# First cross-attention of a two-layer block: queries repeated on four 32-row bands, softmax sums from ACT's accumulator

## What is computed

```python
Ql = (Q @ Wq.T + bq).reshape(b, tq, H, HD).transpose(0, 2, 1, 3)
Kl = (K @ Wk.T + bk).reshape(b, tk, H, HD).transpose(0, 2, 1, 3)
scores = jnp.einsum('bhqd,bhkd->bhqk', Ql, Kl) / scale
scores = jnp.where(key_padding_mask[:, None, None, :], neg_inf, scores)
attn = jax.nn.softmax(scores, axis=-1)
out = jnp.einsum('bhqk,bkd->bqhd', attn, V).reshape(b, tq, H * dv)
return out @ Wo.T + bo
...
x = x + _L0_xattn_ref(_layernorm(x, axis=-1), ctx_1024, ctx_1024, ...)
x = x + _L0_ffn_ref(_layernorm(x, axis=-1), ...)
x = x + _L1_xattn_ref(_layernorm(x, axis=-1), ctx_1024, mask_BxS_ik0, ...)
x = x + _L1_ffn_ref(_layernorm(x, axis=-1), ...)
```

## Time and profile before

| | us |
|---|---|
| median of 3 runs | 433.37 (432.72 to 433.51) |
| the profiled execution | 433.3 |
| its span, first to last instruction | 431.1 |
| busy PE / DVE / ACT / POOL | 384.4 / 296.1 / 174.7 / 90.8 |
| stage A, scores(0) to the last tile added | 16.8 to 85.7 |
| stage C, scores(0) to the last tile added | 308.2 to 416.6 |

### The profile page before, as it was taken

The page is one execution under the profiler, slowest core; times in us unless marked ns, Lnnn a source line. Parts: engine busy times, 40 slices in busy tenths (PEclk is TensorE's granted clock), DMA queues, the critical chain, the costliest instruction groups (busy, mean ns, idle before and its releaser), DMA issues.

```text
span 431.1 us, 6269 instructions
## 1 busy us (share of the span) xinstructions
PE 384.4 (89%) x2440; PEld 255.2 (59%) x2440; DVE 296.1 (69%) x662; ACT 174.7 (41%) x257; POOL 90.8 (21%) x87
## 2 busy tenths in 40 slices
PE   2888998998899499989989999999897899998856
PEld 0445777864555245444444666666475788877745
DVE  5678889485998857634324433344589999999766
ACT  1144442655232045566662222222324244444674
POOL 9004445000501300001000000000025344444500
PEclk9999998999999659999999999999999999999996
DMA  5460000037873000035000000000000000000001
GB/s 160 145 151 0 0 2 0 2 104 220 263 204 100 9 0 2 2 119 185 1 2 0 2 0 2 0 1 2 0 2 0 2 0 2 0 2 0 2 2 49
DMA packets 14864, 18.69 MB, mean 43 GB/s; under 512 B 2485, under 2 KB 11885, under 8 KB 14829
## 3 DMA queue, kind: packets, MB, share of 16 engines
q1 hardware_dynamic: 13634, 17.25, 13.6%
q10 hardware_dynamic: 1200, 1.05, 0.7%
HBM read 12.84 MB, written 5.34 MB: 42 GB/s over the span
## 4 chain that ended last, share of the span: by engine, by line
PE 65%; DVE 25%; issue 4%; ACT 2%; DMA 2%; POOL 1%; SPq 1%; POOLq 0%; DVEq 0%
PE PS L1037 60%; DVE mB L687 4%; DVE usum L534 4%; PE PS L1095 3%; DVE mraw L526 3%; DVE big L543 3%; DMA big<-in_A_WkT 1%; DVE big L858 1%; DVE XN L512 1%; ACT big L983 1%; PE PS L1046 1%; DVE stats L501 1%; DVE nm L671 1%; PE PS L1284 1%; DVE umax L530 1%
## 5 line engine op out<-in xcount | busy, mean ns | idle before, releaser
L1037 PE MATMUL PS<-big 128*128 128x128 f32 (+10 forms) x686 | 121.5, 304 | 13.8 <-DVE mB L687 7.2
L1037 PEld LDWEIGHTS PS<-big 128*128 128x128 f32 (+4 forms) x686 | 78.7, 162 | 55.6 <-ACT big L983 15.0
L888 ACT ACTIVATE big<-PS 128x1280 f32<-128x1280 f32 (+4 forms) x36 | 35.6, 998 | 86.7 <-PE PS L1095 70.3
L438 POOL TENSOR_TENSOR big<-big,urec 128x1024 f32<-128x1024 f32 x24 | 45.6, 1899 | 102.2 <-DVE urec L536 102.2
L687 DVE TENSOR_REDUCE mB<-PS 128x2 f32<-128x256 f32 (+5 forms) x86 | 51.1, 648 | 14.6 <-PE PS L1037 13.9
L983 ACT ACTIVATE big<-PS 128x1024 f32<-128x1024 f32 (+3 forms) x64 | 42.6, 703 | 40.2 <-PE PS L1037 40.0
L1037 PE MATMUL PS<-XT,big 128*128 128x512 f32 x128 | 57.2, 595 | 0.0
L1037 PE MATMUL PS<-cstb 128*128 128x128 bf16 x256 | 51.6, 230 | 0.0
L526 DVE TENSOR_REDUCE mraw<-PS 128x3 f32<-128x462 f32 (+1 forms) x72 | 40.1, 582 | 13.8 <-PE PS L1037 12.0
L762 DVE TENSOR_TENSOR big<-big,PS 128x512 f32<-128x512 f32 x32 | 21.8, 686 | 40.1 <-ACT big L992 39.7
L426 POOL TENSOR_TENSOR rstd<-ve,minus_half 128x4 f32<-128x4 f32 (+2 forms) x13 | 13.0, 1006 | 169.5 <-DVE ve L507 169.4
(11 more groups left out here) (142 smaller groups left out, 456.5 us busy)
## 6 DMA issues: line engine op xcount, KB each, us to landing
scr_qk<-big SPq DMA_DIRECT2D x12, 384.0 KB, 3.6
big<-scr_qk SPq DMA_DIRECT2D x16, 288.0 KB
big<-in_wv SPq DMA_DIRECT2D x1, 2048.0 KB, 8.3
X<-in_x ACTq DMA_DIRECT2D x2, 256.0 KB, 3.5
big<-in_A_WoT ACTq DMA_DIRECT2D x1, 512.0 KB, 5.7
cw<-in_C_Wk SPq DMA_DIRECT2D x1, 512.0 KB, 3.8
cw<-in_C_Wv SPq DMA_DIRECT2D x1, 512.0 KB, 4.7
cw<-in_C_WqT SPq DMA_DIRECT2D x1, 512.0 KB, 6.6
```

The costliest lines, as they stand in the source:

```text
L438: pool.tensor_tensor(pn[:, 0:GH * P].rearrange("p (h k) -> p h k", h=GH), Pt[u % 3][:, :, 0:KM], r.to_broadcast([P, GH, KM]), ALU.mult).th ...
L888: return act.activation(dst, src, ACT.Copy, scale=scale)
L1037: return pe.matmul(o, lhsT, rhs, start=start, stop=stop)
```

## The change

- The queries of stage A are computed: PE multiplies XT by `wq4`, in which Wq's 32 columns stand at rows 4 to 11 of each of four 32-row bands, 8 to a band, that is two heads; ACT scales them and adds the bias into `Q4` (`queries_A`). `K4` holds on each band the keys of its two heads side by side (154 each), zeros for the other head's rows, and the mask in the band's row 0, against which Q4's row 0 is one.
- Scores(u) are four f32 products of 308 columns, one for a band, in PSUM banks 0 to 3. The folds to `kkA`, the key bias, its split, its DMA and the bf16 products go. Turned blocks are in banks 4 to 6, output products in bank 7, and the layer norm of stage B for the first sequence uses bank 3.
- Eight small DMAs on ACT's queue load `own4`; SP loads the mask to all partitions.
- DVE's stage A is a function of its own, `units_A`: one maximum over four banks, umax, two shifts, the reciprocal of u-1, then `add_tile(u-4)`.
- In stages A and C the exponential is eight ACTIVATEs, one a head, each with the sum of its row written to `usum`; the sum on DVE goes.

```diff
-        kkA = c.f32(B * UW).rearrange("p (b n) -> p b n", b=B)
+        K4 = c.f32(B * 2 * KEYS).rearrange("p (b j k) -> p b j k", b=B, j=2)
+        Q4 = c.f32(B * T).rearrange("p (b t) -> p b t", b=B)
...
+        Q4_BANK = (2, 7)
+        LN_B_BANK = (3, LN_BANK)
+        T_BANK = {"A": 4, "C": 3}
+        OUT_BANK = {"A": 7, "C": 6}
+        SHIFTS = {"A": 2, "C": 3}
...
-            sp.wait_ge(part8_ready, 1)
-            for a in range(3):
-                sp.dma_start(browb[32 * a:32 * a + 1].rearrange("p h b k -> p h (b k)"),
...
+            def units_A(between={}):
+
+                for u in range(NT + 1):
+                    if u < NT:
+                        s = PS[:, 0:4, 0:2 * KEYS].rearrange("p g (j k) -> p g j k", j=2)
+                        dve.wait_ge(scores_mm["A"], 4 * (u + 1))
+                        own(dve.tensor_reduce(mraw[:, u % 2, :].rearrange("p (g j) -> p g j", j=2), s, AX.X, ALU.max))
+                        own.wait()
+                        own(dve.tensor_scalar(umax[:, u % 2, :], mraw[:, u % 2, :], LEAST, None, ALU.max))
+                        own.wait()
+                        if u >= 3:
+                            dve.wait_ge(unit_norm["A"], 2 * (u - 2))
+                        for k in range(2):
+                            m = umax[:, u % 2, 4 * k:4 * k + 4].rearrange("p (g j) -> p g j", j=2)
+                            dve.scalar_tensor_tensor(
...
+                    if u >= 1:
+                        v = u - 1
+                        dve.wait_ge(unit_exp["A"], v + 1)
+                        dve.reciprocal(urec[:, v % 3, :], usum[:, v % 3, :]).then_inc(unit_rec["A"], 1)
+                    if u >= 4:
+                        add_tile("A", u - 4)
+                    if u in between:
+                        between[u]()
...
-                        own(dve.tensor_reduce(usum[:, v % 3, :], Pt[v % 3], AX.X, ALU.add))
-                        own.wait()
...
+            dve.wait_ge(ld_own, 16 * 8)
+            dve.wait_ge(zeroed, Z_EARLY)
+            dve.tensor_scalar(s4, e4, -0.5, 0.5, ALU.mult, ALU.add).then_inc(s4_ready, 1)
+            dve.scalar_tensor_tensor(b4, own4[:, 0:1], 0.5, e4, ALU.mult, ALU.add).then_inc(s4_ready, 1)
+            own(dve.tensor_scalar(r4, e4, NEG, None, ALU.mult))
+            dve.wait_ge(wq_mm, 1)
+            dve.tensor_copy(wq4_own, PS[:, 1, 0:HA * HDA].rearrange("p (g r) -> p g r", g=4)).then_inc(wq_ready, 1)
...
+                        for h in range(GH):
+                            i = act.activation(Pt[u % 3][:, h, :], Pt[u % 3][:, h, :], ACT.Exp,
+                                               accum_out=usum[:, u % 3, h:h + 1])
+                        i.then_inc(unit_exp[st], 1)
...
+            for g in range(4):
+                r = slice(32 * g + ROW0, 32 * g + ROW0 + 8)
+                act.dma_start(own4[r, 0:2], t_in["vec"][8 * g:8 * g + 8, V_BQ:V_BQ + 2]).then_inc(ld_own, 16)
+                act.dma_start(own4[r, 2:4], t_in["vec"][8 * g:8 * g + 8, V_HM + 2 * g:V_HM + 2 * g + 2]).then_inc(ld_own, 16)
...
-                            if st == "A":
-                                i = mm(o, onesb[:], browb[:, h0:h1, b, :], start=False)
-                            i.then_inc(scores_mm[st], 1)
+                                pe.wait_ge(unit_shift["A"], 2 * u)
+                            for g in range(4):
+                                r = slice(32 * g, 32 * g + 32)
+                                mm(PS[:, g, 0:2 * KEYS], Q4[r, b, t * P:t * P + P], K4[r, b]).then_inc(scores_mm["A"], 1)
```

More of the change, by code:

```diff
@@ L45 @@
 EPS = 1.0e-5
+LEAST = -3.0e38
 MASK_NEG = 1.0e6
@@ L170, in program @@
         woT = c.f32(HA * D)
[L171 to L182, removed]
+        at = c.at
+        wk4, wq4, own4 = c.f32(P), c.f32(P), c.f32(4)
+        zeroA = big[:, at:c.at]
+        wqA = c.f32(D, HA * HDA)
+        wk4_own, wq4_own = (w.rearrange("p (g r) -> p g r", g=4)[:, :, ROW0:ROW0 + 8] for w in (wk4, wq4))
+        e4, s4, b4, r4 = c.f32(1), c.f32(1), c.f32(1), c.f32(1)
+        mask_words = c.f32(B * KEYS // 4).bitcast(I32)
+        masku = mask_words.bitcast(U8).rearrange("p (b k) -> p b k", b=B)
         assert c.at <= BIGW, c.at
@@ L321, in program @@
         U_LNC, U_LND = 5, 2 * QT + 6
-        PREA = ([("kk", 0, k) for k in range(3)] + [("vw", 0, k) for k in range(2)] + [("kk", 1, k) for k in range(3)]
-                + [("vr", 0, 0)] + [("vw", 1, k) for k in range(2)] + [("vr", 1, 0)])
+        PREA = [(kind, b, k) for b in range(B) for kind, k in (("vw", 0), ("vw", 1), ("vr", 0))]
         def max_parts(m):
@@ L559, in _ @@
[L559 to L573, removed]
-            own(dve.scalar_tensor_tensor(bias8, PS[0:HA, 1, 0:B * KEYS], 0.5, mrow, ALU.mult, ALU.add))
-            own.wait()
-            parts = part8.rearrange("p a b k -> p a (b k)")
-            own(dve.tensor_copy(parts[:, 0], bias8))
-            own.wait()
-            own(dve.tensor_tensor(rest8, bias8, parts[:, 0], ALU.subtract))
@@ new lines, in _, with keys_by_head @@
+            dve.wait_ge(wq_mm, 1)
+            dve.tensor_copy(wq4_own, PS[:, 1, 0:HA * HDA].rearrange("p (g r) -> p g r", g=4)).then_inc(wq_ready, 1)
+            def keys_by_head():
+                dve.wait_ge(k4_mm, 1)
+                dve.wait_ge(ld_mask, 16)
+                for j in range(2):
+                    own(dve.tensor_scalar(K4[:, :, j, :], PS[:, 0, 0:B * KEYS].rearrange("p (b k) -> p b k", b=B),
+                                          own4[:, 1:2], own4[:, 2 + j:3 + j], ALU.add, ALU.mult))
+                own.wait()
+                for j in range(2):
+                    dve.scalar_tensor_tensor(K4[:, :, j, :], masku, r4, K4[:, :, j, :], ALU.mult, ALU.add).then_inc(k4_ready, 1)
@@ L893, in ln_out @@
                     act.wait_ge(ln_turned[name], b + 1)
+                    bank = LN_B_BANK[b] if name == "b" else LN_BANK
                     if w is None:
-                        copy(dst[:, b, :], PS[:, LN_BANK, :]).then_inc(ln_T[name], 1)
+                        copy(dst[:, b, :], PS[:, bank, :]).then_inc(ln_T[name], 1)
                     else:
-                        act.activation(dst[:, b, :], PS[:, LN_BANK, :], ACT.Identity,
+                        act.activation(dst[:, b, :], PS[:, bank, :], ACT.Identity,
                                        scale=w, bias=bias).then_inc(ln_T[name], 1)
@@ L917, in copy_A @@
                     kind, b, k = PREA[m]
-                    bank = 3 + m % 3
-                    act.wait_ge(preA_mm, 1 + m + 1)
-                    if kind == "kk":
-                        h0, h1 = BANK_HEADS[k]
-                        copy(kkA[:, b, h0 * KEYS:h1 * KEYS], PS[:, bank, 0:(h1 - h0) * KEYS], 0.5).then_inc(preA_act, 1)
-                    elif kind == "vw":
+                    bank = 4 + m % 3
+                    act.wait_ge(preA_mm, m + 1)
+                    if kind == "vw":
                         copy(vwAm[:, b, 512 * k:512 * k + 512], PS[:, bank, :]).then_inc(preA_act, 1)
@@ L926, in copy_A, with queries_A @@
                         copy(vwAr[:, b].rearrange("p g o -> p (g o)"), PS[:, bank, 0:2 * D]).then_inc(preA_act, 1)
+            def queries_A(b):
+                act.wait_ge(s4_ready, 2)
+                act.wait_ge(q4_mm, b + 1)
+                act.activation(Q4[:, b, :], PS[:, Q4_BANK[b], :], ACT.Identity, scale=s4, bias=b4).then_inc(q4_ready, 1)
             def copy_C(n0, n1):
```

125 lines of the change are left out of this document (64 added, 61 removed).

## The result

The changed kernel takes 442.67 us (median of four runs, 442.17 to 444.6) against a median of 433.44 for the kernel before on the same chip. By the medians it is slower by 9.2 us; the ratio of the means is 1.0225, interval 1.0191 to 1.0259. The forecast was 437.7, slower by 4.4. The profiled execution took 443.1 us with a span of 441.3; against the 431.1 of before that is +10.2 of span, where my terms come to +4.4. One run of all, the fourth of e7, took 451.18 us at a mean granted clock of 0.842 where the other three have 0.959 to 0.967, a slower state of the chip; it is left out of e7's figures.

The account below looks back on a forecast made before the run. PE, busy for 89% of the span, was taken to bound the kernel. 433.3 - 0.6 (stage A at full clock) + 10 (PE's clock) - 5 (stage C) = 437.7 us, range 427.5 to 449.

Parts of the forecast that it names:

- Scores on bands: Stage A's scores: four f32 products of 308 columns overlap on row bands, 0.65 us, saving 1.95 us of PE a unit.
- rival 3: Stage A: the bands don't overlap, scores take 2.1 to 2.5 us; total 445 us, chance 0.08.
- Eight exponentials: ACT in stages A and C: eight exponentials with written sums take 2.7 us, where one took 1.22.
- Rival 2: ACT in stages A and C: the written sum is dear, 4.0 us for the eight; total 451 us, chance 0.12.
- The start: Ahead of stage A's first scores: scores(0) begin at 15.2 in place of 16.82, 1.6 us earlier.
- Units 0 to 3, and with them scores(4): Stage A: these units take about 8, 4.1, 3.9 and 4.7 us; scores(4) start at about 35.9, not 44.31.
- The serial step: Stage A from unit 4: PE's products wait for add_tile at the end of DVE's unit; 7.8 us a unit against 5.92.
- The clock: Stage A, units 4 to 8: PE's clock falls with idles of some 3.8 us; 2 us a unit, +10 us.
- Behind scores(7): End of stage A: scores(7) at 59.3, products(5) at 71.5, last tile added at 85.0 at the full clock.
- Stage C: Second cross-attention: 1.43 us a unit leaves DVE's road, 5.0 of PE's 6.3 us idle comes back; -5 us.
- Behind the last scores 0: End of stage C: 2.7 us of exponentials replace 1.22 + 1.43, so no change.

Follow-up runs that it names:

- e7: The e1 kernel with GpSimd's clearing of its weights held until VectorE has normalised all tiles; 418.45 us, 0.9645 of the kernel before.
- e1: The changed kernel with stage A's add of tile u-4 moved to the head of unit u, ahead of the maxima; 418.64 us, ratio 0.9654.
- e11: The e1 kernel with e7's wait, identity products in PE's waits of unit 2, and two last-layer relus behind the copy of PT; 414.17 us.
- e5: The changed kernel, order untouched, with eleven identity products in PE's wait ahead of stage A's products of units 4 to 8; 435.81 us, ratio 1.0044.
- e6: The kernel before with one part alone: eight exponentials with sums written by ScalarE in stage C, stage A as before; 426.84 us, ratio 0.9857.
- e12: The changed kernel with five identity products in PE's wait ahead of stage A's products of units 4 to 8; 437.06 us, ratio 1.0055.

## Why the prediction was wrong in its size

The direction, the mechanism and the range (427.5 to 449) hold; the size is half of what it was. By my own steps:

- *Scores on bands*: 0.65 us forecast, 0.80 measured. Right; rival 3 is out. From the start of the scores to that of the next product it is 0.73 us (25.27 to 26.00 in the changed kernel). The rule of the Trainium skill that I weighed (TensorEngine Tiling (Array Packing), Key Properties: a change of tiling mode drains the engine) isn't seen as a cost of its own in that.
- *Eight exponentials*: 2.7 us forecast; a step from one to the next is 0.31 us, and the eight take 2.6 with the last sum (51.15 to 53.75). Rival 2 is out, though its premise is half true: the written sum is a record of its own (0.19 us), but it lies beside the end of its exponential and the start of the next one. That the price of an operand fitted was luck: no row had shown such a sum.
- *The start*: scores(0) at 15.2 forecast, 16.45 measured. The normalising was priced alone. The longest of these instructions took 2.11 us, the median 0.34, while POOL cleared weights beside it; e7 shows the pair. The Trainium skill, SBUF — State Buffer, Who interferes with whom, has it that a `tensor_scalar` in a two-port mode and a GpSimd instruction shut each other out for a whole instruction; the trace agrees that they do, 2.68 us against 1.10 (that these ran in this mode no trace shows). But here it was for longer than one: the first of the four started at 8.75 and ended at 10.86, just behind the last of four clearings on POOL (10.78), and not behind the one that ran when it began (7.73 to 9.54).
- **Units 0 to 3, and with them scores(4)**: this is the step that failed. "Scores(4) starts at about 35.9" was 40.29, 4.4 of the 5.8 us by which the span missed. 1.25 is the start, 1.0 units 0 and 1 (8.8 and 4.3 against 8 and 4.1), and 2.1 units 2 and 3, which took 10.74 us, not 8.6, since the clock was low in them: turnings 2.4 us and products with scores 4.91. I had let the clock fall in units 4 to 8 only, where the idles are long, and put it at nothing here, where idles of 0.99 and 1.69 us (in e1 a third of 0.45) lie close together. With the clock up, e7 has 8.65 us for these two units; with both causes gone, e11 has scores(4) at 35.91, to the hundredth my figure only by luck, since it starts at 14.76 and not 15.2. What made unit 0 longer stands below the list.
- *The serial step*: 7.8 us a unit at the full clock forecast, 7.97 in e5. Right. Two roads of nearly the same length, too: exponentials end at 53.75, shifts at 54.04.
- *The clock*: 2 us a unit forecast, 1.68 measured up to scores(7), and 28.96 us from scores(4) to scores(7) against 29.4. In units 7 and 8 it is 2.4 each, by the next point. Five units make 9.9 us, my estimate from these figures, against 10: right in sum.
- *Behind scores(7)* 29.7 forecast, 30.9 measured to the last tile. 0.8 of the 1.2 us is the clock: from 73.80 and from 84.10 on twenty products took 4.4 us from start to start, where e1 has 2.3, and the turnings 0.3 more than there, 2.4 a unit in place of 2. The other 0.4 is open.
- *Stage C*: -5.0 forecast, -4.35 measured, by two errors that nearly cancel. In front of the last scores it gained 6.8 us: PE's idle behind the shifts went from 6.3 to 0.5 us, more than I let it. "Behind the last scores 0" was +2.45: 0.8 for the late copy and 1.6 for the clock that fell there. e6, where it didn't fall, tells the two apart.

The 0.8 us by which unit 0 was longer than forecast is PE's speed too. The folds of unit 0, first in the changed kernel, then in e12, whose unit 0 took 7.96 us:

```profile
21.52 3.82 PE L1063 MATMUL PS<-big,ctxT 128*128 128x512 f32 x20
```

```profile
21.55 2.96 PE L1063 MATMUL PS<-big,ctxT 128*128 128x512 f32 x20
```

They begin at half speed, though the granted clock reads 1.00: in the changed kernel their records of 512 columns start 0.86 us apart up to 24.08, and the eight of 512 columns from 100.64 on start 0.43 apart. The moment at which they speed up differs between executions. The twenty take 2.96 to 4.48 us, and that is the whole spread of unit 0.

4.4 - 0.4 + 1.2 + 0.65 is 5.85, the 5.8 us of span within rounding; the time outside the span was 0.4 us less than before.

## What to carry to other kernels

When an edit moves a small step on one engine, ask which instruction of another engine waits for it, and count all that now stands ahead of it: 0.24 us of addition, moved behind 3.3 us of other work, cost 24 us. When PE waits more, look for its clock in every stretch with waits, the short ones close together too, and not only in the longest; products whose result nobody reads, put into the wait, can tell what the clock costs. A gain by a faster engine in front of the last unit has to be followed to the end of the program, where its new length may stand ahead of something else.

## What the runs showed of the hardware

- ACT's sum of an exponential's row is a record of its own, `ACTIVATION_READ_ACCUMULATOR`, 0.19 us for 128 x 1. With it an exponential over 154 columns takes 0.31 us from start to start; eight take 2.6 us with the last sum, where one over all 1232 takes 1.22.
- Four f32 products on four 32-row bands, 308 columns each, run beside one another in 0.80 us at the full clock and in 1.41 at half (34.36 in the changed kernel, granted clock 0.50). Scores(0) took 1.41 us too, at 16.45, where the granted clock reads 1.00: in the first 24 us this column doesn't show at what speed PE runs, and the lengths of its records do.
- PE's clock doesn't follow from the length of one idle stretch: 1.67 us with a fall in three units and without in one of the same execution (e12), 2.16 us with a fall in five executions and without in four, 1.96 us with a fall in e11 and without in e1, the same three short idles with a fall in e1 and without in e7. Such a kernel's own runs spread: e1's five are 3.5 us apart, where nine of the kernel before are within 1.9. What decides it is left open.
